# Attention in one core: the weighted sum of V over two key tiles at a time instead of one, with the order of all engines made anew

## What is computed

```python
qkv = einsum('bnd,ed->bne', x, qkv_w) + qkv_b          # x: 4 x 512 x 128
attn = softmax(einsum('bhqd,bhkd->bhqk', q, k) * SCALE) # 16 heads of 8 channels
out  = einsum('bhqk,bhkd->bhqd', attn, v)
x = layernorm(x + (out @ fc_w.T + fc_b + x))
h = silu(tlin(x, w1)) * tlin(x, w2)                     # 128 -> 512
h = gelu(tlin(h, h1))                                   # 512 -> 512
h = gelu(tlin(h, h2))                                   # 512 -> 512
x = layernorm(x + tlin(h, w3))                          # 512 -> 128; tlin is (h @ w.T) * s
```

## Time and profile before

| | |
|---|---|
| time, median of 3 runs | 326.8 us (326.24 to 327.55) |
| profiled execution | 328.06 us, of which 326.2 us are the span from the first to the last instruction |
| PE busy | 302.8 us (93% of the span) |
| DVE busy | 247.5 us (76%) |
| ACT busy | 235.1 us (72%) |
| POOL busy | 148.0 us (45%) |
| mean granted clock of PE | 0.955 |

### The profile page before, as it was taken

How to read it: one execution, slowest core, us unless ns; L and a number is a source line. 1 busy time by engine, 2 the same in 40 slices (tenths; PEclk the granted TensorE clock), 3 DMA queues, 4 the chain that set the end, 5 groups by cost and what they waited for, 6 DMA issues and landing times.

```text
span 326.2 us, 5521 instructions
## 1 busy us (share of the span) xinstructions
PE 302.8 (93%) x1780; PEld 137.9 (42%) x1780; DVE 247.5 (76%) x516; ACT 235.1 (72%) x433; POOL 148.0 (45%) x227
## 2 busy tenths in 40 slices
PE   8665999999998999999999999999999997999991
PEld 7531123222332333423543435335434351489990
DVE  3769799999989998789987688677774800079974
ACT  3553568988767998798679996897699889438340
POOL 6284039911143891119708992261398805320101
PEclk9895799999999999999999999999999999699996
DMA  6444443132211221311040204020100010000011
GB/s 142 171 103 69 68 157 94 29 53 34 44 25 43 40 36 16 52 30 23 1 74 10 44 12 78 0 44 9 34 2 0 1 34 0 4 0 2 0 34 37
DMA packets 17830, 13.44 MB, mean 41 GB/s; under 512 B 2551, under 2 KB 16648, under 8 KB 17800
## 3 DMA queue, kind: packets, MB, share of 16 engines
q1 hardware_dynamic: 17546, 12.85, 19.0%
q10 hardware_dynamic: 254, 0.20, 0.3%
HBM read 5.51 MB, written 1.05 MB: 20 GB/s over the span
## 4 chain that ended last, share of the span: by engine, by line
PE 63%; POOL 11%; DVE 9%; ACT 6%; issue 4%; DMA 3%; SPq 1%; ACTq 1%; POOLq 0%; DVEq 0%
PE bank L445 25%; PE bank L480 14%; PE bank L465 9%; PE bank L456 8%; POOL hT L990 3%; DMA h_nat<-in_L_ffn_h_w_dram 3%; ACT prob L654 2%; DVE negmax L803 2%; PE bank L420 2%; PE bank L503 2%; POOL hT L987 1%; ACT h_nat L729 1%; DVE y L793 1%; PE bank L438 1%; DVE parts L817 1%
## 5 line engine op out<-in xcount | busy, mean ns | idle before, releaser
L803 DVE TENSOR_REDUCE negmax<-bank 128x1 f32<-128x512 f32 x256 | 161.5, 682 | 26.6 <-PE bank L456 26.1
L654 ACT ACTIVATE prob<-bank 128x512 f32<-128x512 f32 x256 | 137.9, 605 | 26.7 <-PE bank L465 26.1
L480 PE MATMUL bank<-prob,v_sb 128*32 128x512 f32 x512 | 75.1, 625 | 2.6 <-ACT prob L654 2.6
L445 PE MATMUL bank<-act,hT 128*128 128x512 f32 (+1 forms) x320 | 71.0, 363 | 0.4 <-POOL act L1013 0.3
L456 PE MATMUL bank<-stack 61*128 61x512 bf16 x256 | 68.4, 395 | 2.9 <-DMA stack<-parts 1.8
L465 PE MATMUL bank<-stack 64*128 64x512 bf16 x256 | 65.6, 388 | 2.2 <-DMA stack<-mT 1.4
L445 PEld LDWEIGHTS bank<-act,hT 128*128 128x128 f32 x320 | 48.3, 190 | 16.6 <-issue 9.7
L456 PEld LDWEIGHTS bank<-stack 61*128 61x128 bf16 x256 | 16.5, 94 | 60.8 <-issue 44.7
L722 ACT ACTIVATE h_nat<-bank,hs_all 128x512 f32<-128x512 f32 (+1 forms) x40 | 22.8, 603 | 24.2 <-PE bank L445 24.2
L465 PEld LDWEIGHTS bank<-stack 64*128 64x128 bf16 x256 | 15.7, 94 | 37.3 <-issue 23.8
L954 POOL TENSOR_TENSOR rstd<-rstd,mhalf 128x4 f32<-128x4 f32 (+1 forms) x10 | 9.7, 970 | 47.9 <-DVE rstd L784 47.8
(11 more groups left out here) (120 smaller groups left out, 347.1 us busy)
## 6 DMA issues: line engine op xcount, KB each, us to landing
stack<-parts SPq DMA_DIRECT2D x124, 48.0 KB
x_in<-in_L_attn_x_dram SPq DMA_DIRECT2D x4, 256.0 KB, 3.0
h_nat<-in_L_ffn_h_w_dram SPq DMA_DIRECT2D x1, 1024.0 KB, 8.5
work<-in_L_ffn_h_w_dram SPq DMA_DIRECT2D x1, 1024.0 KB, 6.1
res<-in_L_attn_x_dram SPq DMA_DIRECT2D x4, 256.0 KB, 2.8
out_dram<-y SPq DMA_DIRECT2D x3, 256.0 KB, 2.3
work<-in_L_ffn_w_w_dram SPq DMA_DIRECT2D x2, 256.0 KB, 3.5
stack<-mT SPq DMA_DIRECT2D x30, 6.0 KB
```

The costliest lines, as they stand in the source:

```text
L445: mm = nc.tensor.matmul(dst, w, v, start=first and n == 0, stop=last and n == len(pairs) - 1)
L480: last = nc.tensor.matmul(space("P", pfirst)[at:at + VW, :], v_sb[b % 2][:, kt, of:of + VW], prob[:, t % NP, :], start=kt == 0 and slot % ...
L654: nc.scalar.activation(prob[:, n % NP, :], space("T", n)[:, :], ACT.Exp, scale=SCALE).then_inc(emptied("T", n), 1)
L803: nc.vector.tensor_reduce(negmax[:, g % 2, col:col + 1], space("S", n)[:, :], AX.X, ALU.max, negate=True).then_inc(emptied("S", n), 1)
```

## The change

`PK` goes from 1 to 2: a P step takes the eight matmuls of two key tiles (four in the group cut in two), and there are 34 such steps instead of 68. The five tables are new. Each holds the same words as often as before, but for one filler `K` that is gone; what has moved is the place of each, and the bank of most PE steps. By its description up to four S, four T and six score tiles hold banks at once. No other line is touched, so lines move up by two.

```diff
 SP_ORDER = """
-lw lh xin vb xin zq*5 zk zq zk zq*2 zk mrow zk*2 lh zk l3 mrow more xres xin spread mrow spread mrow spread mrow spread mrow xres spread mrow spread
+lw lh xin vb zq*4 zk*6 mrow xin zq lh zq*3 l3 mrow more xres spread mrow xin spread mrow spread mrow spread mrow spread xres mrow spread mrow spread
...
 PE_ORDER = """
-x:0 wq:1 q:2 q:3 v:4 wt:5 wt:6 wt:0 x:1 wt:2 wt:3 wt:5 v:1 wf:6 S:0 S:4 S:1 S:6 S:0 S:2 S:4 S:1 S:3 S:6 S:5 S:0 S:2 m:4 S:1 S:3 S:6 S:5 S:4 S:0 S:2
+x:0 wq:1 q:2 q:3 v:4 wt:5 wt:6 wf:0 wt:1 wt:2 wt:3 wt:5 x:6 v:1 S:4 S:0 S:6 S:2 S:3 S:1 S:4 S:0 S:6 S:5 S:2 S:3 S:1 S:4 m:0 S:6 S:5 S:2 S:0 S:3 S:1
...
-    PK = 1
+    PK = 2
```

More of the change, by code:

```diff
@@ L8 @@
 SP_ORDER = """
-lw lh xin vb xin zq*5 zk zq zk zq*2 zk mrow zk*2 lh zk l3 mrow more xres xin spread mrow spread mrow spread mrow spread mrow xres spread mrow spread
-mrow spread mrow spread mrow*2 spread xres mrow spread*2 out mrow spread mrow xres mrow*2 out*4
+lw lh xin vb zq*4 zk*6 mrow xin zq lh zq*3 l3 mrow more xres spread mrow xin spread mrow spread mrow spread mrow spread xres mrow spread mrow spread
+mrow*2 spread mrow xres spread*2 mrow out spread mrow spread xres mrow*3 out*4
 """
 PE_ORDER = """
-x:0 wq:1 q:2 q:3 v:4 wt:5 wt:6 wt:0 x:1 wt:2 wt:3 wt:5 v:1 wf:6 S:0 S:4 S:1 S:6 S:0 S:2 S:4 S:1 S:3 S:6 S:5 S:0 S:2 m:4 S:1 S:3 S:6 S:5 S:4 S:0 S:2
@@ new lines @@
+S:4 T:6 T:5 m:2 S:0 S:6 T:3 T:2 S:5 T:1 S:3 T:4 S:2 T:0 S:1 T:6 P:7 S:4 S:5 T:0 T:6 S:3 P S:2 S:1 T:0 T:4 T:6 S:5 S:3 S:0 T:4 P S:2 S:6 T:1 T:4 S:5
+m:3 S:0 S:1 P S:3 S:2 q:4 q:6 S:5 S:0 S:1 S:3 T:2 T:4 S:2 T:5 T:4 wt:6 wt:0 wt:5 hs:4 wt:6 wt:1 S:0 S:5 S:3 T:6 T:4 S:2 T:6 S:0 T:4 S:5 T:6 S:3 T:4 P
+m:2 S:6 S:0 S:4 T:5 S:2 T:3 S:1 x:6 S:0 T:5 S:4 S:6 T:2 S:3 T:5 T:1 S:2 S:0 T:4 S:5 S:6 T:3 T:1 P T:2 S:0 S:4 S:5 S:3 L:6 m:1 T:0 T:2 T:1 T:4 o:6 T:0
+S:5 S:2 S:3 S:1 S:4 T:5 T:6 P:7 T:0 T:2 T:5 T:3 S:6 S:1 S:0 S:4 S:2 T:6 T:5 T:1 S:3 S:0 P S:6 T:4 S:5 T:1 T:2 m:3 T:4 T:0 S:1 S:3 T:6 T:2 T:5 S:4 S:1
@@ new lines @@
+S:0 T:3 P T:6 S:4 S:2 S:5 S:1 T:3 T:0 S:6 T:4 S:3 T:2 S:0 T:5 T:4 S:1 P S:2 S:5 T:6 T:4 S:3 v:0 m:1 o:6 T:2 T:4 S:1 T:5 T:0 T:2 T:4 S:3 S:6 a:5 q:0
+q:1 S:2 S:3 S:4 S:6 T:5 P:7 S:0 T:2 T:5 f:1 T:2 T:3 T:5 x:1 T:2 T:3 T:5 P T:1 T:4 T:2 S:3 T:6 S:5 S:0 S:1 S:4 T:3 T:2 X:6 P T:3 T:5 T:2 T:0 S:1 S:3
+m:6 S:5 S:4 T:2 S:6 A:1 A:0 A:3 B:2 B:5 S:4 T:1 S:2 S:6 S:0 S:5 T:4 T:1 A:3 B:2 P S:4 S:1 S:6 S:0 T:2 T:5 o:3 S:4 T:2 S:5 T:1 S:2 T:6 T:1 B:3 S:0 S:6
+T:4 T:1 S:3 m:5 H:4 H S:2 S:1 T:5 S:0 T:6 P:7 S:3 S:5 T:2 T:6 H*2 S:1 S:0 S:2 T:3 T:6 S:4 H:5 H S:3 S:1 T:6 T:0 H*2 S:2 S:4 S:6 T:0 T:3 P S:5 S:1 T:0
@@ L35 @@
+m:1 Y:4 P T:6 T:5 T:1 T:0 H:4 o:2 H T:3 T:6 T:5 T:1 H P:7 T:2 T:0 T:3 T:6 H H:5 H*3 T:1 T:2 T:0 T:4 H:3 H*3 H:6 T:5 T:1 T:2 T:0 P T:4 T:3 H*3 T:5 T:1
+T:2 T:0 P T:4 T:3 T:6 P K:0*2 o:5 K:0*2 a:1 a:2 K:0 f:0 H:4 H*3 H:3 H*3 H:6 f:7 X:5 H*3 H:1 H*3 A:2 A:0 A:4 A:3 W:7 X:6 B:5 B:1 W*2 A:2 A:6 A:0 A:5
+B:4 W B:1 B:3 B:2 B:4 B:6 Y:7 H:1035 H*9 H:2467 H*9 H:1035 H*9 H:2467 H*8 W:1 W*3 H K:0 Y:0 W:3 W*2 K:1*2 W K:0 Y:5
 """
 ACT_ORDER = """
[L38 removed]
@@ L42 @@
+e*6 a q*2 e*6 x e*12 m e*2 t*2 u t u e*3 t u o e*6 u e*2 m e*4 h e*4 h e*6 h e*2 h m g m e*9 o e*7 a e m e h e*2 q*2 h*3 e g e t u t u t e t u e u
+e*15 m e w3 e*2 o e*11 h e*3 h e*4 h e m e*2 h g e*11 o e*6 a e*4 h*2 e*2 h e h g m t u t u t*2 u m u e*15 w3 e m e*3 o e*10 h e*2 h e*4 h e*6 h e g
+e*6 wg o a*2 h*4 ws t*6 w3 t*2 wg h*15 w3 h w3
 """
 DVE_ORDER = """
-wq r mid r lo db mid lo db v*2 wf s*40 r s r s lo s lo s*4 hs s*16 wx s*3 L or s om s*31 v or s om s*4 r s l1 lo l1 s l1 s l1 s r s l1 lo s Xh s Xl
@@ L46 @@
[L46 to L49, removed]
+wq r mid r db mid lo db lo v wf v s*42 r s r s lo s lo s hs s*20 wx s*3 L s*2 or s om s*28 v or s om s*3 r s r lo s l1 lo l1 s l1 s l1 s*2 l1 s*2 Xh s
@@ L50 @@
+Xl s*5 t s t s t s*4 t s*2 or s om s*49 v or om l1*4 r l1 r lo*2 s*4 Xh s Xl s*4 t*3 s t s*15 l2*2 s l2 s or l2 om s*2 l2 s*22 or om s*8 l1 s l1*3 s
+l1 s*5 Xh s Xl s*4 t*3 s t s*8 l2*4 or om l2 or om l1*4 gh l1 gl l1 Xh l1 gh l1 gl l1 gh Xl gl l1 gh gl Xh Xl gt h0 gt l0 h0 gt l0 gt h0 gt l0 h0 gt
+l0 gt h0 gt l0 h0 l2 l0 h0 l2 l0 h0 gh l0 gl gh l2 gh l2 gh gl gh gl gh gl gh gl gh gl l2 gh gl gh gl gh gl gh gl*3 gh gl gh*2 gl*2 l2 gh l2 gl l2*8
 """
 POOL_ORDER = """
-vz*2 wc wl wc wl wc wl wc wl wc wl wc m wl m*2 da mid db da mid db wc wl xr m wc wl wc wl wc wl wc wl m*3 da mid db da p1 mid db xr m u h0 l0 u h0 l0
@@ L54 @@
-u h0 l0 m u h0 l0 m*2 gh*4 gl*4 mid*2 da db da db m p1 xr gh gl m gh gl u gh gl gh gl u h0 l0 h0 l0 u*2 h0 l0 h0 l0 m p2 gh*4 gl*4 m p1 m xr gh gl gh
-gl u gh gl u gh gl m h0 u l0 h0 l0 u p2 h0 l0 h0 l0 gh*4 gl*4 p1*2 p2*3
+vz*2 wc*2 wl*2 wc*3 wl*3 wc m wl m*2 da*2 mid*2 db*2 wc xr wc m wl*2 wc*3 wl*3 m*3 da mid da mid db*2 p1 m xr u*2 h0 l0 h0 l0 u h0 m l0 u h0 l0 m*2
+gh*4 gl*4 m p1 da mid da mid db*2 xr gh gl gh gl u*4 gh gl m gh gl h0 l0 h0 l0 h0 l0 h0 l0 p2 m gh*4 gl*3 m gl p1 xr m gh gl u*2 gh gl u gh*2 gl*2 u m
@@ L56 @@
+h0 l0 h0 l0 h0 l0 h0 l0 p2 gh*4 gl*4 p1*2 p2*3
 """
```

32 lines of the change are left out of this document (9 added, 23 removed).

## The result

The changed kernel takes **348.2 us** (median of 4 runs, 346.75 to 352.5) where the kernel before took 326.62 beside it (326.24 to 327.55): 1.064 times the time, 95% interval 1.060 to 1.068. The forecast was 318.8 us and faster. Its profiled execution took 347.76 us, span 346.0, mean granted clock 0.933 (before 0.955).

What follows compares the result with a forecast made beforehand. DVE was taken to bound score tiles 0 to 128, PE the stretches after; -2.9 + 2.1 - 8.0 + 1.3 - 0.5 = -8.0 on the 326.2 us span gave 318.2, plus 0.6 for the median: 318.8 us, range 310.5 to 326.0.

Steps and rivals of the forecast that it cites:

- Prices of the forms: PE's tiling forms: ST pair 0.22 us, leaving ST 0.09; P pass 0.43 plus 0.14 a stay; full-form stay some 0.20.
- The start: Before the first score tiles: SP issues copies some 3.5 us sooner, first S stays near 19.5 us, later ones stop waiting.
- A, -2.9: Score tiles 0 to 64, paced by DVE: 44.0 us instead of 46.9, as S waits for the spread copies go.
- B, +2.1: Score tiles 64 to 128: 53.5 us instead of 51.4, DVE running short of tiles during eight-tile P steps.
- C, -8.0: Score tiles 128 to 255, bound by PE: 119.8 us instead of 127.8, from fewer changes of form and fuller pairing.
- The larger of PE's and DVE's sums: Score tiles 128 to 255 cut into eighths, the slower engine's work counted in each: 116.2 us, plus 3.6 lost as before.
- D, +1.3: From score tile 255 to the third sequence's last first-hidden-layer piece: 24.6 us instead of 23.3, through work moved in.
- E, -0.5: From 268.9 us on: last P step ends 0.9 us sooner, fillers add 1.0, four W steps moved ahead save 0.6.
- the prediction's own signs: Tile 128 after 120 us would mean DVE starves; tiles 128 to 255 taking over 123 us, that evacuation sets the pace.
- both slower ones: DVE starves at P steps before tile 128: 330.2 us, chance 0.10; evacuation also paces tiles 128 to 255: 323.8 us, 0.18.
- The rule on evacuation: Tiling speeds TensorE but not PSUM evacuation; taken to fit score tiles 0 to 128, not yet 128 to 255.
- C does not yet: Claim that score tiles 128 to 255, unlike those before, were not yet paced by evacuation; DVE busy 102.8 of 127.8 us.

## Why the prediction was wrong

- *Prices of the forms.* Right. P steps of 1.86 us, 34 of them 0.3 us off the bare price in all. The bare time of PE did fall by 18 us.
- *The start.* Right in kind: SP issues its copies from 11.21 us instead of 15.82, no S waits for them any more, the first S starts at 18.56 (19.5 forecast).
- *A, -2.9.* It came out at +0.4. DVE is busy for 41.7 of 47.3 us. PE's waits for the spread went, but DVE still waits 4.7 us for S tiles: 1.9 us had been left for both the start and the P steps.
- *B, +2.1.* It came out at +9.4. DVE idles 9.4 us of the stretch (51.4 busy of 60.8). The term let DVE starve only while PE is in P, and as if the order offered as many tiles as the banks allow.
- *C, -8.0.* **The step that failed**: it came out at +9.5. "The larger of PE's and DVE's sums" over eighths of 16 tiles takes for granted that the two can drift apart by a sixteenth of the program. They can drift by seven banks. Within one P stay and one row of S and T neither engine can work ahead. First PE is away and DVE and ACT run dry, then PE issues a pair each 0.22 us and its readers need 0.60 for one S tile. C has 14.1 us of excess in ST stays, 9.8 of it in five long ones, and up to 7.2 of clock on a bare 114.2.
- *D, +1.3 and E, -0.5.* +2.3 and -0.9. In E the parts were off: the wait ahead of the last P step was 5.92 us (2.35 before), and the step ended 8.0 us after the second table load (294.15 to 302.1), not 7.
- *The rivals.* By the prediction's own signs both slower ones held: tile 128 came at 126.7 (after 120), and C took 137.3 (over 123). Each was priced as if the other did not hold. Together (+11.4 and +5.0 on -8.0) they give some 335 us, 13 short of the result. No case had the lower clock outside the last P step; it can be at most 10.6 of the 13, and some 3 are shown. What makes up the rest is open. With the rivals priced apart, the range ended at 326.
- *The rule on evacuation* (the Trainium skill, "TensorEngine Tiling (Array Packing)", "PSUM Bottleneck") spoke for this result, and was set aside with "C does not yet". The runs agree with it: halving both readers' work took 12.0 of the 21.1 us away.

**What is shown and what is not.** Shown by runs: the merge alone loses 18 us; merging costs more where it makes rows of S and T long (1.018 against 1.006); cutting long rows in 15 places gives 6.6 us back; the readers' pace is more than half of it; the table pauses, the eighth exponential and the ring are not; filling the waits brings the clock back and 3 us of time. Not shown: what the new order costs by itself, since taking 30 pairs apart in it gave nothing; why a pair merged at short rows still loses 0.3 us; why the clock fell in the new order and not in the old; and how the loss divides between banks and clock, for which there is only the account. That the hand-made orders tried here do not gain says nothing of the best order for merged P steps.

## What to carry to other kernels

A cheap, dull step between two rows of matmuls may be the time in which the readers empty the banks. Before packing such steps together, count the tiles in a row between two of them and set them against the banks: in this kernel rows of seven tiles or more, at seven banks, cost 0.14 us a tile more, and what the fewer changes of form saved was given back. A bound as the larger of two engines' sums is safe only over stretches as short as the buffers between them.

## What the runs showed of the chip

In the changed kernel part of the time ran at the lower clock. The windows show a granted clock of 0.94 between 60 and 303 us, and the timeline shows a row of S and T at DVE's pace (153.72, 154.32, 154.92, 155.52) and right behind it a P step at the lower of the two levels, 1.2 GHz, 3.50 us from start to start in place of 1.86:

```profile
153.72 0.39 PE L454 MATMUL bank<-stack 61*128 61x512 bf16 x1 [0.29 <-DVE negmax L801]
154.32 0.39 PE L454 MATMUL bank<-stack 61*128 61x512 bf16 x1 [0.21 <-DVE negmax L801]
...
159.36 3.57 PE L478 MATMUL bank<-prob,v_sb 128*32 128x512 f32 x16
162.86 0.39 PE L454 MATMUL bank<-stack 61*128 61x512 bf16 x2
```

Such a row is not enough for it. Before, four rows of 7 to 10 tiles in B, each 0.3 to 0.7 us over its price, left the clock at 1.00. In the changed kernel rows of 14, 11 and 15 tiles between 78 and 94 us, each 1.2 to 1.5 us over, left it at 1.00 too, and the merge alone in the old order kept 0.99. What tells the rows apart is not shown.
